# Earlier loads of C, a longer run of condition matmuls ahead of a stack, and other PSUM banks at the group boundary of a scan layer

## The chip, the core and the metric

The kernel runs on one core of a Trainium2 chip. The metric is the time of one execution in microseconds of the device. Five engines work side by side and wait for each other through semaphores: TensorE (PE, with its weight loads as PEld), VectorE (DVE), ScalarE (ACT), GpSimd (POOL) and SyncE (SP), which issues most of the DMAs.

## The reference, cut to what matters

The input x has 32 batches of 64 steps and 1024 channels. The layer is

```
c   = x @ W + lora(x)                     # "cond", gathered adapters, 1024 x 1024
dt, B, C = projections of c               # dt of 1024 channels, B and C of 16 states
h_t = exp(dt*A) * h_(t-1) + dt*B*c        # 16 states of each channel, 64 steps
y   = sum over states(h_t * C_t) + D*c
x1  = x + y
out = x1 + gated low-rank delta of (x1 @ W2 + bias + lora)
```

The part that the change touches is the scan `h` and the product `h * C`.

## The kernel before

The 32 batches are cut into 8 **groups** (G0 to G7) of 4 batches, that is 256 tokens. A group has 8 channel blocks `j` of 128 channels, and a block has 4 **units** `un`, each 8 states by 128 tokens. A place in the order is written (j, un), and a group has 32 of them, 256 in all. At each unit

- PE makes `dBx` (function `b_times_dtx`, four matmuls of `Bd` with `stacked`) in one of two PSUM buffers; it waits until the scan two units back is done;
- DVE scans it into `h` (L1011); it waits for `dBx`, for the decays `dA` (ACT, L612), and, `h` having two slots, for the product of two units back;
- POOL multiplies `h` by `Cb`, which is C spread over all partitions, into `hC` (L578);
- PE sums `hC` of three units back over the states (`sum_states`, L1214, eight transposing matmuls into bank `yp[j % 2]`, called "Y").

All the rest is cut into **jobs** that a table gives to a unit: `JOBS` for G1 to G5, `FIRST` for G0, `SIXTH` (jobs of at most the next group) for G6 and `FINAL` for G7. A job has a PSUM bank: "A" and "B" are `jb[0]` and `jb[1]`, "Y" is the `yp` of the block. PE does the jobs of a unit in the order of the list, after `b_times_dtx` and `sum_states` of that unit. It waits before the first matmul of a job until the bank's last tenant has been read. ACT does its part of a `stack`, `dtz` or `cond` one unit later (`LATE_ON_ACT`), DVE its part of a `dtz` one unit later (`LATE_ON_DVE`), its part of a `stack` or `xr` at the same unit, after the scan.

The jobs at the boundary:

- `cond` i of a later group, by chunks of k: three matmuls of 256 columns for each of 8 chunks, then one with the adapter (and, for i = 0, it needs `low`, which comes out of `xr`). Blocks 2m and 2m+1 share bank A.
- `dtz` i: two matmuls, then a softplus (ACT L593, L595, L597) and a max-add on DVE (L813) give the **step size** `dt` of two blocks.
- `xr`: 16 matmuls, then DVE L914 makes `low`.
- `stack` i: two transposes of `dtx` (made by POOL, L558, after the `hC` of the unit in the table `DTX`: `dtx` 8 at (6,3), 9 at (7,0), 2 at (0,0)). ACT copies them (L637), DVE subtracts (L906), SP writes them out (`put_dtx`, L421, 256 KB), waits for the landing, and at the next unit reads them back as `stacked` (`stack_dtx`, L428, three loads of 128 KB). `stack` 8 and 9 are blocks 0 and 1 of the next group.
- `b_diagonals` (DVE L829) makes `Bd` of the next group, at (6,3), (7,1), (7,3) and (0,1).

C of the next group is written to DRAM by SP at (6,2) (`put_c`, four DMAs, L406) and read back, spread over the partitions, by `spread_c` (L416): one load of 512 KB for each `un`. `Cb` has four slots, one for each `un`, so the load of slot un waits for the last `hC` of the group before that reads it, at (7, un). The loads of un 0, 1 and 2 are issued at (7,1), (7,2) and (7,3), that of un 3 at (0,1) of the next group. POOL waits for each of them at the first four units of a group. SP does everything in one order, so a wait in it holds what stands behind.

Of the kernel before, what the change touches and what calls it, by code (L numbers as in the profile page):

```python
# [4 lines left out]
P = 128  # L5
# [16 lines left out]
ROWS = 3 * Q  # L22
NDA, NH, NHC, NDT = 2, 2, 4, 4
PARTS = ((0, 0), (0, 1), (1, 0))
# [9 lines left out]
def job(name, i, bank, ks=None, ahead=None):  # L34
# [34 lines left out]
    (6, 3): [],  # L69
    (7, 0): [job("xr", 0, "Y", (0, 4)), job("xr", 0, "Y", (4, 8)), job("stack", 8, "B")],  # L70
    (7, 1): [job("cond", 0, "A", (0, 4), 2), job("dtz", 5, "Y")],
    (7, 2): [job("cond", 0, "A", (4, 8), 2), job("stack", 9, "B")],
    (7, 3): [job("cond", 1, "A", (0, 1), 2)],
}
# [29 lines left out]
    (6, 3): [],  # L104
    (7, 0): [job("xr", 0, "Y", (0, 4)), job("xr", 0, "Y", (4, 8)), job("stack", 8, "B")],
    (7, 1): [job("cond", 0, "A", (0, 4), 2), job("dtz", 5, "Y")],
    (7, 2): [job("cond", 0, "A", (4, 8), 2), job("stack", 9, "B")],
    (7, 3): [job("cond", 1, "A", (0, 1), 2)],
}
# [13 lines left out]
LORA_A, LORA2, LORA_B, LORA2_B = range(4)  # L123
ADAPTERS = {(1, 2): LORA2_B, (3, 0): 0, (4, 0): 1, (5, 2): 2}
DIAGONALS = {(0, 1): 3, (6, 3): 0, (7, 1): 1, (7, 3): 2}


def layer_kernel(nc, x, ids1, ids2, W, loraA, loraB, A_log, Dw, xproj_w, dtproj_w, dtproj_b,
# [6 lines left out]
    with ctx:  # L135
# [40 lines left out]
        Bd = sb("Bd", [P, NQ, R, Q], fr)  # L176
        Cb = sb("Cb", [P, UNITS, UNIT])
        x1 = sb("x1", [P, 2, TT, D])
# [27 lines left out]
        def xT_of(part, i):  # L206
# [4 lines left out]
               x1T[:, 4:8, :].rearrange("p k t -> p (k t)"), x1[:, 0, 0, :], x1[:, 0, 1, :], hC[:, 1, :], hC[:, 2, :], hC[:, 3, :]]  # L211
        Wraw = [Cb[:, :, :].rearrange("p u c -> p (u c)").rearrange("p (k o) -> p k o", k=K // 2),
                dA[:, :, :].rearrange("p h c -> p (h c)").rearrange("p (k o) -> p k o", k=K // 2)]
# [119 lines left out]

        def times_C(un):
            return (hC[:, un % NHC, :].rearrange("p (n b t) -> p b n t", n=HS, b=2),
                    h[:, un % NH, :].rearrange("p (b n t) -> p b n t", n=HS, b=2),
                    Cb[:, un, :].rearrange("p (b n t) -> p b n t", n=HS, b=2))

# [25 lines left out]
        def _(sp_e):  # L364
# [46 lines left out]
            def spread_c(G, un):  # L411
                if un == 0:
                    wait(sp_e, cscr_out, 64 * G + 64)
                wait(sp_e, hC_made, UNITS * K * G - UNITS + un + 1)
                src = c_scratch[G]
                sp_e.dma_start(Cb[:, un, :], src[un:un + 1, :].to_broadcast([P, UNIT])).then_inc(C_in[un], 16)  # L416

# [57 lines left out]
            def body(G, par):  # L475
                last = G == GROUPS - 1
                first = G == 0
                two_more = G + 2 < GROUPS
                for j in range(K):
                    t = K * G + j  # L480
                    for un in range(UNITS):
                        if un == 0:
                            load_xres(G, j, t)
                        if (j, un) == (0, 1) and not first:
                            spread_c(G, UNITS - 1)
                        which = ADAPTERS.get((j, un))
                        if which == LORA2_B:
                            load_lora2_b(G)
                        elif which == LORA2:
                            load_lora2(G)  # L490
                        elif which == LORA_A and two_more:
                            load_lora_a(G + 2)
                        elif which == LORA_B and two_more:
                            load_lora_b(G + 2)
                        for name, i, g, gpar, psum in ended_before(G, par, j, un):
                            if name == "stack":
                                stack_dtx(g, i)
                        for name, i, g, gpar, psum in ended_at(G, par, j, un):
                            if name == "stack":
                                put_dtx(g, i)  # L500
                        for name, i, g, gpar, psum in ended_at(G, par, j, un):
                            if name == "Bst":
                                put_c(g)
                            if name == "out":
                                store(g, i)
                        if j == K - 1 and un >= 1 and not last:

                            spread_c(G + 1, un - 1)

# [11 lines left out]
        def _(pool):  # L521
# [44 lines left out]
            def body(G, par):  # L566
                first, final = (G == g for g in (0, GROUPS - 1))
                for j in range(K):
                    for un in range(UNITS):
# [7 lines left out]
                        ns = slice(0, HS // 2 if s + 1 == UNITS * K * GROUPS else HS)  # L577
                        pool.tensor_tensor(*(x[:, :, ns, :] for x in times_C(un)), ALU.mult).then_inc(hC_made, 1)  # L578
                        if (j, un) in DTX and not (final and DTX[j, un] >= K):
# [229 lines left out]
        def _(dve):  # L809
# [218 lines left out]
            dve.wait_ge(C_in[UNITS - 1], 16 * GROUPS)  # L1028
            dve.tensor_tensor(*(x[:, :, HS // 2:, :] for x in times_C(UNITS - 1)), ALU.mult).then_inc(last_half, 1)
            add_residual(G, G % 2, K - 1, K * GROUPS - 1)  # L1030
# [312 lines left out]
```

## Time and profile before

| | us |
|---|---|
| median of 3 runs | 911.11 |
| lowest and highest | 909.5 and 913.29 |
| the profiled execution, its own time | 908.23 |
| its span, first to last instruction | 906.0 |
| busy: PE, DVE | 806.1 (89%), 764.7 (84%) |
| busy: POOL, ACT | 688.2 (76%), 643.4 (71%) |

The profile is of one execution, which was 2.9 us shorter than the median. 2.2 us of its time lie outside of the span. TensorE's granted clock was 0.968 of 2.4 GHz on the mean. The loop over the groups runs from 69.3 us to 885 us. A group takes 102.7 to 105.9 us from its first scan to that of the next one, G6 101.1.

### The profile page before, as it was taken

To read this page: it belongs to the slowest core of one execution; us is meant where nothing else is said; L and a number is where in the kernel's file an instruction comes from. 1 tells how busy PE (TensorE), PEld (TensorE's weight loads), DVE (VectorE), ACT (ScalarE), POOL (GpSimd) and SP (SyncE) were. 2 spreads that over 40 slices of the span, in tenths; PEclk is the share of its full clock that TensorE was granted. 3 is DMA by queue.
4 is the path that set the end of the run, shared out by engine and by line. 5 is a ranking of instruction groups with operands and counts; after the bars stand their busy time and mean duration, and the time that the engine had idled before them with its cause. 6 is when DMAs were issued, how large, how long until landed. Compare 5 with 4: busy or idle time off the path is not lost.

```text
span 906.0 us, 18640 instructions
## 1 busy us (share of the span) xinstructions
PE 806.1 (89%) x6416; PEld 770.7 (85%) x6416; DVE 764.7 (84%) x688; ACT 643.4 (71%) x1489; POOL 688.2 (76%) x349
## 2 busy tenths in 40 slices
PE   5988999899988999799988999799998999578784
PEld 4988998889978998799988998799987899567772
DVE  3447789888997899898998899988998799999993
ACT  4656678677775877777786886778776786779750
POOL 2016788788787888888878887788878898799891
PEclk9997999999998999999999999999999999899998
DMA  9988777366656557475675757375664754253221
GB/s 251 388 329 268 233 238 211 135 218 184 211 160 226 190 170 238 122 273 149 206 214 178 247 158 247 121 251 167 213 192 148 221 172 141 70 163 101 88 64 47
DMA packets 103113, 172.24 MB, mean 190 GB/s; under 512 B 21865, under 2 KB 71657, under 8 KB 94830
## 3 DMA queue, kind: packets, MB, share of 16 engines
q1 hardware_dynamic: 85614, 94.12, 34.1%
q10 hardware_dynamic: 17408, 76.95, 24.7%
q8 instruction: 53, 0.87, 0.4%
q14 instruction: 38, 0.31, 0.1%
HBM read 137.33 MB, written 33.69 MB: 189 GB/s over the span
## 4 chain that ended last, share of the span: by engine, by line
PE 52%; POOL 12%; DVE 11%; issue 10%; ACT 9%; DMA 5%; SPq 0%; POOLq 0%; ACTq 0%; DVEq 0%
PE jb L1047 24%; PE yp L1214 13%; POOL hC L578 10%; PE dBx L1047 7%; DVE h L1011 6%; ACT dA L612 4%; PE jb L1051 3%; PE yp L1047 3%; DMA Cb<-c_scratch 2%; POOL dtx L558 2%; DMA dtx_scratch<-HL 1%; DVE Bd L829 1%; DMA x<-in_x 1%; PE yp L1051 1%; PE yp L1219 1%
## 5 line engine op out<-in xcount | busy, mean ns | idle before, releaser
L578 POOL TENSOR_TENSOR hC<-h,Cb 128x1024 f32<-128x1024 f32 (+1 forms) x256 | 632.5, 2475 | 145.0 <-DVE h L1011 130.6
L1011 DVE TENSOR_TENSOR_SCAN h<-dA,dBx 128x1024 f32<-128x1024 f32 x256 | 583.4, 2281 | 62.1 <-PE dBx L1047 50.3
L612 ACT ACTIVATE dA<-dt,negA 128x252 f32<-128x252 f32 x1024 | 430.3, 494 | 75.5 <-DVE h L1011 65.2
L1214 PE MATMUL yp<-ident,hC 128*128 128x128 f32 x2048 | 274.7, 278 | 16.7 <-DVE HL L906 8.0
L1214 PEld LDWEIGHTS yp<-ident,hC 128*128 128x128 f32 x2048 | 236.7, 144 | 20.7 <-issue 11.4
L1047 PE MATMUL jb<-xT,Wst 128*128 128x256 f32 x1416 | 215.7, 296 | 0.0
L1047 PE MATMUL dBx<-Bd,stacked 96*128 96x256 f32 x1024 | 186.1, 304 | 12.8 <-DVE h L1011 6.2
L1047 PEld LDWEIGHTS jb<-xT,Wst 128*128 128x128 f32 x1416 | 186.2, 195 | 1.9
L1047 PEld LDWEIGHTS dBx<-Bd,stacked 96*128 96x128 f32 x1024 | 146.2, 195 | 18.8 <-issue 15.6
L558 POOL TENSOR_TENSOR dtx<-dt,u 128x256 f32<-128x256 f32 x64 | 54.2, 847 | 39.2 <-DVE dt L813 39.2
L647 ACT ACTIVATE u<-jb 128x512 f32<-128x512 f32 x31 | 18.6, 599 | 33.1 <-PE jb L1047 30.7
L829 DVE TENSOR_TENSOR Bd<-Bhl,diag 96x1024 fp32r<-96x1024 f32 x32 | 38.6, 1208 | 0.1
L1047 PE MATMUL jb<-low,GB 128*128 128x256 f32 x128 | 38.2, 379 | 0.0
L910 DVE TENSOR_TENSOR xT<-jb,xT 128x512 fp32r<-128x512 f32 x26 | 17.8, 684 | 21.3 <-ACT xT L641 21.1
L1219 PE MATMUL yp<-ident,Du 128*128 128x128 f32 x128 | 35.7, 279 | 0.0
L639 ACT ACTIVATE x1T<-jb 128x512 f32<-128x512 f32 x32 | 19.1, 596 | 22.4 <-PE jb L1051 21.7
L1047 PE MATMUL jb<-G,x1T 128*128 128x132 f32 x256 | 33.7, 279 | 1.0 <-ACT x1T L639 0.7
L641 ACT ACTIVATE xT<-jb 128x512 fp32r<-128x512 f32 x26 | 15.5, 596 | 26.8 <-PE jb L1051 26.2
L1051 PE MATMUL jb<-ident,dtx 128*128 128x128 f32 x48 | 9.7, 284 | 26.0 <-POOL dtx L558 26.0
L1047 PEld LDWEIGHTS jb<-G,x1T 128*128 128x128 f32 x256 | 30.8, 190 | 1.8 <-ACT x1T L639 0.9
L603 ACT ACTIVATE Du<-u,Dsb 128x256 f32<-128x256 f32 x64 | 31.6, 496 | 0.0
L1047 PE MATMUL jb<-u,xprojT 128*128 128x256 f32 x128 | 30.5, 381 | 0.7 <-ACT u L647 0.7
(173 smaller groups left out, 735.3 us busy)
## 6 DMA issues: line engine op xcount, KB each, us to landing
Wst<-W_scratch ACTq DMA_DIRECT2D x54, 1024.0 KB, 5.9
stacked<-dtx_scratch SPq DMA_DIRECT2D x192, 128.0 KB, 2.6
dtx_scratch<-HL SPq DMA_DIRECT2D x64, 256.0 KB, 3.1
Cb<-c_scratch SPq DMA_DIRECT2D x32, 512.0 KB, 5.7
xres<-in_x SPq DMA_DIRECT2D x64, 128.0 KB, 4.3
out<-obuf SPq DMA_DIRECT2D x32, 256.0 KB, 3.9
xin<-in_x ACTq DMA_DIRECT2D x26, 256.0 KB, 5.2
GB<-in_L_cond_lora_B SPq DMA_DIRECT2D x64, 64.0 KB, 5.6
```

Source lines behind the costliest of these rows:

```text
L558: pool.tensor_tensor(dtx[:, i % 2, :], dt[:, i % NDT, :], u[:, i % K, :], ALU.mult).then_inc(dtx_made, 1)
L578: pool.tensor_tensor(*(x[:, :, ns, :] for x in times_C(un)), ALU.mult).then_inc(hC_made, 1)
L603: act.activation(Du[:, i % 4, :], u[:, i % K, :], ACT.Copy, scale=Dsb[:, i % K:i % K + 1]).then_inc(Du_made, 1)
L612: act.activation(dA[:, half % NDA, :].rearrange("p (b n t) -> p b n t", b=GB_, n=HS)[:, :, n, 1:STEPS], dt[:, j % NDT, :].rearrange("p (b ...
L639: act.activation(x1T[:, 2 * i:2 * i + 2, :].rearrange("p k t -> p (k t)"), psum[:, :], ACT.Copy).then_inc(taken[name], 1)
L647: act.activation(u[:, i - 1:i + 1, :].rearrange("p k t -> p (k t)"), psum[:, :], ACT.Copy).then_inc(taken[name], 1)
L829: dve.tensor_tensor(Bd[0:ROWS, NQ // 2 * p:NQ // 2 * (p + 1), HS * half:HS * (half + 1), :], Bhl[0:ROWS, NQ // 2 * p:NQ // 2 * (p + 1), HS ...
L1011: dve.tensor_tensor_scan(h[:, un % NH, :], dA[:, half % NDA, UNIT * p:UNIT * (p + 1)], dBx[un % 2][:, :], 0.0, ALU.mult, ALU.add).then_inc ...
L1047: return pe.matmul(o, lhsT, rhs, start=start, stop=stop, **kw)
L1051: return pe.matmul(o, in_, ident[first:first + n, first:first + n], is_transpose=True, start=True, stop=True)
L1214: last = pe.matmul(y, hC[:, un % NHC, P * n:P * (n + 1)], ident[:, :], is_transpose=True, start=un == 0 and n == 0, stop=False, skip_group ...
L1219: last = pe.matmul(y, Du[:, j % 4, P * p:P * (p + 1)], ident[:, :], is_transpose=True, start=False, stop=True, skip_group_check=True)
```

## The change

`Cb` gets seven slots, used in a ring: unit un of group G has slot (4G + un) mod 7. The loads of the next group are issued at (6,3) (un 0 and 1), (7,0) (un 2) and (7,1) (un 3), each after the other SP work of its unit. The wait of a load is that of the slot's reader in the ring: for un 0 to 2 a product of a whole group ago, for un 3 the product at (7,0). The load at (0,1) is gone. At (7,0) the two halves of `xr` go to bank B instead of Y, then come five chunks of `cond` 0, which used to stand at (7,1), and then `stack` 8, now in bank Y instead of B. `dtz` 5 at (7,1) goes to bank B instead of Y, with one chunk of `cond` 0 behind it (before it were four); (7,2) has two chunks instead of four; `stack` 9 moves from (7,2) to (7,3), behind the one chunk of `cond` 1, in bank B as before. G6 has neither `xr` nor the chunks, but does have `stack` 8 in Y, `dtz` 5 in B and `stack` 9 at (7,3). A scratch area that the build reserves for DMA is halved, which makes room for the slots.

```diff
-NDA, NH, NHC, NDT = 2, 2, 4, 4
+NDA, NH, NHC, NDT, NCB = 2, 2, 4, 4, 7
...
# in JOBS and in FIRST alike
-    (7, 0): [job("xr", 0, "Y", (0, 4)), job("xr", 0, "Y", (4, 8)), job("stack", 8, "B")],
-    (7, 1): [job("cond", 0, "A", (0, 4), 2), job("dtz", 5, "Y")],
-    (7, 2): [job("cond", 0, "A", (4, 8), 2), job("stack", 9, "B")],
-    (7, 3): [job("cond", 1, "A", (0, 1), 2)],
+    (7, 0): [job("xr", 0, "B", (0, 4)), job("xr", 0, "B", (4, 8)), job("cond", 0, "A", (0, 5), 2), job("stack", 8, "Y")],
+    (7, 1): [job("dtz", 5, "B"), job("cond", 0, "A", (5, 6), 2)],
+    (7, 2): [job("cond", 0, "A", (6, 8), 2)],
+    (7, 3): [job("cond", 1, "A", (0, 1), 2), job("stack", 9, "B")],
...
+SPREAD = {(6, 3): (0, 1), (7, 0): (2,), (7, 1): (3,)}
...
-        Cb = sb("Cb", [P, UNITS, UNIT])
+        Cb = sb("Cb", [P, NCB, UNIT])
...
+        def C_slot(G, un):
+            return (UNITS * G + un) % NCB
...
-                wait(sp_e, hC_made, UNITS * K * G - UNITS + un + 1)
+                s = UNITS * G + un - NCB
+                if s >= 0:
+                    sp_e.wait_ge(hC_made, UNITS * K * (s // UNITS + 1) - UNITS + s % UNITS + 1)
                 src = c_scratch[G]
-                sp_e.dma_start(Cb[:, un, :], src[un:un + 1, :].to_broadcast([P, UNIT])).then_inc(C_in[un], 16)
+                sp_e.dma_start(Cb[:, C_slot(G, un), :], src[un:un + 1, :].to_broadcast([P, UNIT])).then_inc(C_in[un], 16)
...
-                        if (j, un) == (0, 1) and not first:
-                            spread_c(G, UNITS - 1)
...
-                        if j == K - 1 and un >= 1 and not last:
-
-                            spread_c(G + 1, un - 1)
+                        for ahead in SPREAD.get((j, un), ()) if not last else ():
+                            spread_c(G + 1, ahead)
...
-    nc = _bacc.Bacc("TRN2", target_bir_lowering=False, num_devices=1, dynamic_dma_scratch_size=1024)
+    nc = _bacc.Bacc("TRN2", target_bir_lowering=False, num_devices=1, dynamic_dma_scratch_size=512)
```

## Rows read from the trace of the kernel before

**Rows 1.** Waits of all engines: who waited for whom, us in total, times, longest
```profile
PE jb L1051 <- POOL dtx L558: 26.0, 7, 6.8
...
POOL hC L578 <- DMA Cb<-c_scratch: 4.8, 3, 2.9
```

**Rows 2.** Timeline of PE, boundary of G3 and G4: start, us, what
```profile
472.86 2.15 PE L1047 MATMUL yp<-xT,GAs 128*128 128x256 f32 x16
477.97 0.41 PE L1051 MATMUL jb<-ident,dtx 128*128 128x128 f32 x2 [2.96 <-POOL dtx L558]
...
480.25 2.60 PE L1047 MATMUL jb<-xT,Wst 128*128 128x256 f32 x12
...
488.17 0.64 PE L1047 MATMUL dBx<-Bd,stacked 96*128 96x256 f32 x4
...
489.44 2.03 PE L1047 MATMUL jb<-xT,Wst 128*128 128x256 f32 x15
...
497.87 0.41 PE L1051 MATMUL yp<-ident,dtx 128*128 128x128 f32 x2 [1.48 <-POOL dtx L558]
```

**Rows 3.** A stretch: us, busy of PE, PEld, DVE, ACT, POOL, then PEclk, DMA share
```profile
478.00:484.00 6.00, 6.00 (x39) 6.00 (x40) 4.18 (x5) 3.20 (x8) 5.34 (x3) 0.72 0.33 107
```

**Rows 4.** Timeline of DVE there; L1011 are the scans, from (7,1) to (0,0)
```profile
474.86 0.68 DVE L813 SCALAR_TENSOR_TENSOR dt<-jb,dt 128x512 f32<-128x512 f32 x1
...
479.18 2.28 DVE L1011 TENSOR_TENSOR_SCAN h<-dA,dBx 128x1024 f32<-128x1024 f32 x1
...
483.60 2.29 DVE L1011 TENSOR_TENSOR_SCAN h<-dA,dBx 128x1024 f32<-128x1024 f32 x1 [1.03 <-PE dBx L1047]
...
487.30 0.42 DVE L906 TENSOR_TENSOR HL<-jb,HL 128x256 fp32r<-128x256 f32 x1 [0.82 <-ACT HL L637]
487.64 0.41 DVE L819 TENSOR_TENSOR x<-yp,xres 128x256 f32<-128x256 f32 x1
487.97 2.28 DVE L1011 TENSOR_TENSOR_SCAN h<-dA,dBx 128x1024 f32<-128x1024 f32 x1
...
491.28 2.27 DVE L1011 TENSOR_TENSOR_SCAN h<-dA,dBx 128x1024 f32<-128x1024 f32 x1
```

**Rows 5.** Timeline of DVE, boundary of G6 and G7: the scans (7,1) and (0,0)
```profile
787.88 2.29 DVE L1011 TENSOR_TENSOR_SCAN h<-dA,dBx 128x1024 f32<-128x1024 f32 x1
...
797.95 2.27 DVE L1011 TENSOR_TENSOR_SCAN h<-dA,dBx 128x1024 f32<-128x1024 f32 x1
```

**Rows 6.** Landing of three loads of stacked, issued at 481.5; then at 274.8
```profile
DMA to landing us min/median/max: 2.4/2.9/3.9
...
DMA to landing us min/median/max: 2.4/2.6/5.3
```

**Rows 7.** Timeline of SP's queue, boundary of G3 and G4
```profile
479.35 0.34 SPq L421 DMA_DIRECT2D dtx_scratch<-HL  x1
481.53 1.26 SPq L428 DMA_DIRECT2D stacked<-dtx_scratch  x3
```

**Rows 8.** Stretches (0,0) to (3,0) of G2, G3, G1, G6; one in G7
```profile
282.63:321.61 38.98, 38.98 (x322) 38.34 (x321) 31.06 (x21) 25.80 (x61) 30.68 (x17) 0.93 0.62 208
388.54:424.32 35.78, 34.27 (x301) 33.42 (x300) 30.95 (x22) 27.80 (x65) 32.47 (x17) 1.00 0.65 218
178.00:214.44 36.44, 34.62 (x301) 33.46 (x300) 30.88 (x22) 27.94 (x65) 32.42 (x17) 1.00 0.66 210
696.81:733.42 36.61, 34.74 (x301) 33.48 (x300) 30.87 (x22) 27.97 (x65) 32.45 (x17) 1.00 0.69 218
806.60:810.00 3.40, 3.40 (x19) 3.40 (x18) 2.33 (x2) 2.17 (x5) 3.13 (x4) 0.50 0.31 109
```

**Rows 9.** Timeline of PE: dBx at (0,0) of G2; stack 2 in G7
```profile
281.40 1.20 PE L1047 MATMUL dBx<-Bd,stacked 96*128 96x256 f32 x4 [3.53 <-DVE Bd L829]
...
804.53 0.41 PE L1051 MATMUL yp<-ident,dtx 128*128 128x128 f32 x2 [2.46 <-POOL dtx L558]
```

**Rows 10.** The page, DMA issues: count, KB each, us to landing
```profile
Cb<-c_scratch SPq DMA_DIRECT2D x32, 512.0 KB, 5.7
```

## What the change does to the time: the prediction

> **What bounds the kernel now.** I read the page first, then the waits of all engines, then the timeline of PE, DVE and SP around one boundary, then stretches of equal content. The page has PE at 89% and no engine idle for long, so it names no single bound; the waits do better. The largest one of PE in the loop is that for `dtx` from POOL in front of a `stack` in a `jb` bank: 26.0 us in 7 times, that is one wait at each of the seven boundaries, the largest (6.8) in G6 where PE has least to do [rows 1]. The timeline of PE at the boundary of G3 and G4, which stands for those of G0 to G5, shows it: `xr` ends at 475.0, and PE does nothing until `stack` 8 at 477.97 [rows 2]. After that idle stretch the granted clock is at its lower level, 1.2 GHz, for some 3.4 us: the stretch 478 to 484 has a mean of 0.72, where 1.2 GHz all through would be 0.50, and 12 `cond` matmuls take 2.60 us there, while 15 of the same take 2.03 at 2.4 GHz [rows 2, 3]. So PE loses about 3.0 us of idle time and about 1.5 us to the clock at each boundary, 4.5 in all.
>
> What PE loses isn't yet what the kernel loses. The other clock to read is the chain of scans on DVE [rows 4]. From the scan at (7,1), 479.18, to the one at (0,0), 491.28, are 12.10 us. The scan at (7,2) stood 1.03 us waiting for `dBx` from PE, which was busy with the four slow chunks of `cond` 0, and L906 stood 0.82 us waiting for ACT, which had waited for PE. In G6, whose (7,1) and (7,2) have no chunks, but `dtz` 5, both stacks and the same DVE work, the same stretch takes 10.07 us, 787.88 to 797.95 [rows 5]. That is a chain of DVE alone, and it is the floor for what the change can reach.
>
> **The change part by part.**
>
> *Five chunks ahead of `stack` 8.* Fifteen matmuls, 2.03 us [rows 2], go into the 2.96 us in which PE waits. They need bank A, whose tenant `dtz` 4 is read by L813 from 474.86 to 475.54 [rows 4], so PE starts them at about 475.6 and ends at 477.6, before `dtx` is there (477.9). `stack` 8 is not later; the margin is 0.3 us, and below it each 0.1 us costs 0.1 us. What stays idle is 0.6 and 0.3 us, in two pieces, and no low clock should follow. Bank Y for `stack` 8 has been free since the residual of block 5, a unit before; `xr` in B finds it free.
>
> *Fewer chunks behind.* (7,1) has 3 `cond` matmuls instead of 12, (7,2) 6 instead of 12. PE's `dBx` for (7,2) then comes at about 481, and DVE goes by its own work: scan and diagonals 3.31 us (as 487.97 to 491.28), so (7,2) at 482.5 instead of 483.6. Then scan, L813 and L819: about 2.2 + 0.65 + 0.4 = 3.25, so (7,3) at 485.75 instead of 487.97. Then scan, diagonals and now L906, 3.31 + 0.35, so (0,0) at 489.4 instead of 491.28 [rows 4]. Gain: 1.9 us, where the row of G6 gives 2.03 [rows 5]. Bounds: 2.0 above; below, 1.0, if only the wait for `dBx` goes and L906 meets a late ACT at its new place.
>
> *`stack` 9 a unit later.* Its bank B waits for L813 of `dtz` 5, which ends at about 485.5, and PE may stand some 0.8 us there. It is needed at (1,0), four units on. The put follows at about 490 and the loads at about 492.5, with no C load beside them; 2.4 to 5.3 us to land [rows 6] leaves room before 501. Cost nothing. In G6 the move puts 0.35 us of L906 from (7,2) to (7,3), and I count +0.3 for it.
>
> *Does the gain last?* Behind (0,0), PE must reach `stack` 2 when `dtx` 2 is there, and `dtx` 2 hangs on the scan at (0,0) through POOL. PE had 1.48 us of idle time there [rows 2]; from `dBx` of (0,0) at 488.17 it needed 8.2 us to be ready. With `dBx` at 486 to 487 it is ready at 494.2 to 495.2, and `dtx` 2 comes at 496.0. So PE doesn't bind before, and behind it everything is relative to `stack` 2. Six boundaries (G0 to G5) give 6 x 1.9 = 11.4 us; bounds 6 to 12.
>
> *C earlier.* SP's waits at (6,3) are for `put_c` to land, some 2.5 us at a time when its next urgent work (the put of `dtx` 8, 479.35) is 6 us off [rows 7]. The stalls for C that it removes: POOL's named waits are 4.8 us in 3 times [rows 1], but most of it is made up by slack. From (0,0) to (3,0), where the jobs are the same, G3 (0.3 us of such a wait) takes 35.78 us, G1 (2.7) takes 36.44, G6 (2.9) 36.61 [rows 8]. So 0.7 + 0.8 = 1.5 us come back, and nothing in G2 to G5. Bounds 0 and 4.8.
>
> *`stack` 8 behind a C load.* This is the cost to weigh. The third C load is now issued about 0.4 us behind the put of `dtx` 8 and ahead of the three loads of `stacked`. Those had landed 3.9 us after the third issue at most, 486.2, with PE asking at 488.17 [rows 2, 6, 7]. PE would now ask at 486.0 (the wait for L813 to 485.5, then the two transposes of `stack` 9), but by the slack just worked out it may be kept until about 488. I take the C load to cost them 1 us (its 512 KB against their 384), so they land at about 487, at no price. Bounds: nothing, and 2.4 us more than the 5.3 which the boundary of G1 and G2 shows.
>
> By the Trainium skill's "DMA: Bandwidth & Descriptors", section "Queues, rings and completion order", each DMA engine takes descriptors in ring order, so all of the C load stands in front of the `stacked` loads. The trace before has no such order at this place; the rule makes rival 3 likelier.
>
> *Sum.* 908.23 of the profiled execution - 11.4 - 1.5 + 0.3 = 895.6. The median of the runs is 2.9 us above that execution, so 898.5. I add 2 us for boundaries where a load comes late or the clock falls once: 900.5. A difference under 0.5% (4.6 us) can't be told from none here.
>
> **Rivals.**
>
> 1. *The gap moves to `stack` 2.* PE keeps 4.5 us and the chain only 1.9, so 2.6 more stand somewhere: partly before `stack` 9 and `dBx` of (0,0), partly before `stack` 2. An idle stretch of 1.5 us there left the clock up in G1 to G6, one of 2.46 us in G7 was followed by 3.4 us at 0.50 [rows 8, 9]. Behind `stack` 2 scans wait for PE, so a low stretch there costs about 1.5 us, and takes back most of the 1.9. At all six: 908.23 - 6 x 0.4 - 1.5 + 2.9 = 907 to 908, no difference. For it: the sizes; against it: the idle time is split.
> 2. *More than the sum.* At the boundary of G1 and G2 a load of `stacked` took 5.3 us. PE waited 3.53 us for it, and from (0,0) to (3,0) G2 took 38.98 against 35.78 us, at a mean clock of 0.93; ahead of (0,0) I estimate 1.6 of the 3.53 as lost too [rows 6, 8, 9]. If the new order avoids this, 4.8 more: about 894.
> 3. *Slower: `stacked` behind the C load.* It decides from a landing 1.8 us later than the 486.2 of before, that is 488. If the loads land at 490, PE stands 2 us past its slack and the clock falls behind that, as with the 3.53 us wait at 281.4 [rows 8, 9]: 2 + 1.6 against a gain of 1.9, +1.7 us at each of six, -1.5 for C: about 920. Against it: a whole load of C takes 5.7 us to land [rows 10], and would be down at 485.5.
> 4. *It does nothing.* Bank A free too late, so that the chunks push `stack` 8 by what they save later. It takes a start after 476.5; L813 is a fixed 0.7 us behind the diagonals, so I see no cause. About 909.
> 5. *All that PE loses comes back.* If DVE's chain didn't cap it, 4.5 us at each of six boundaries: 908.23 - 27 - 1.5 + 0.3 + 2.9 = 883. Against it: the 10.07 us of G6, where PE had nothing to do at all [rows 5].
>
> The Trainium skill speaks for rival 5 and prices it much the same ("TensorE: Matmul & The Clock Gate", section "HAM oscillation — how this bites in real kernels"): time at the lower clock costs half of itself, and the wait ahead of it comes on top. For the 3.4 us here that is an estimate of 1.7 by the page, beside the 1.5 by the rows.
>
> **How the numbers follow.** Forecast 900.5 with 0.58, its own range 895 to 905; rival 1, with a part of the boundaries, 0.17; rival 2, 0.1; rival 3, 0.08; rival 4, 0.05; rival 5, 0.02. Faster by over 0.5% is below 906.6: the forecast, rivals 2 and 5 and a part of rival 1, 0.74. Within: most of rival 1, rival 4: 0.17. Slower: rival 3 and a bit of the unknown, 0.09. The range 893 to 909 leaves out rivals 3 and 5 and the ends.
>
> **What would show it.** Right: in PE's timeline 15 matmuls between `xr` and `stack` 8, no low clock at 478 to 482; (7,1) to (0,0) about 10.2 us; no wait of POOL for C; a wait before `stack` 2 of 1 to 2 us at full clock. Wrong: a wait of `dBx` at (0,0) for `stacked`; a low clock behind `stack` 2; `stack` 8 later against the scan at (7,0) than 2.5 us.

## The result, and the profile after

| | before | after |
|---|---|---|
| median, us (20 runs each) | 912.57 | 920.39 |
| lowest and highest | 907.13 and 917.38 | 910.66 and 927.92 |
| ratio of after to before, 95% | | 1.0068 [1.0044, 1.0091] |

The change makes the kernel 0.7% slower. The forecast was 900.5 us, its range 893 to 909: the time lies outside of it, at rival 3's 920. The four longest runs of after, those above 924 us, are left out of the ratio; with them the medians are 7.8 us, 0.9%, apart. The profiled execution of after took 927.92 us, 7.5 above its median; what is read from it below was also seen at the boundaries of other kernels, the twelfth above all, whose profiled execution took 922.87.

The page of after, span and busy times:

```profile
span 925.7 us, 18639 instructions
...
PE 817.6 (88%) x6416; PEld 780.4 (84%) x6416; DVE 764.2 (83%) x688; ACT 641.0 (69%) x1489; POOL 688.4 (74%) x349
```

DVE and POOL do the same work in the same time. PE has 11.5 us more of it for the same 6416 matmuls, and its granted clock was 0.948 on the mean, where it was 0.968. The waits say what the clock follows (who waited for whom, us in total, times, longest):

```profile
DVE h L1014 <- PE dBx L1050: 76.5, 79, 4.1
...
PE dBx L1050 <- DMA stacked<-dtx_scratch: 30.9, 9, 5.9
...
PE yp L1054 <- POOL dtx L561: 8.9, 8, 5.2
```

The wait that was to go, PE's for `dtx` in front of `stack` 8, was 26.0 us before [rows 1]. `stack` 8 is in bank Y now, so it is in the last row: 7.4 of these 8.9 us, and 5.25 of them in G6. POOL's wait for `Cb` (4.8 us before) isn't in the list any more. In their place stand 30.9 us in which PE waits for `stacked` to land, and 24.0 of these are six waits of 2.96, 5.40, 4.37, 5.88, 2.92 and 2.50 us at (0,0) of G1 to G6. DVE's wait for `dBx` has grown with it, from 50.3 us in 68 times to 76.5.

The timeline of PE at the boundary of G3 and G4 (start, us, what, idle time before), the counterpart of [rows 2]:

```profile
480.96 2.05 PE L1050 MATMUL jb<-xT,Wst 128*128 128x256 f32 x15 [1.16 <-DVE dt L816]
483.40 0.41 PE L1054 MATMUL yp<-ident,dtx 128*128 128x128 f32 x2 [0.39 <-POOL dtx L561]
...
490.82 0.44 PE L1054 MATMUL jb<-ident,dtx 128*128 128x128 f32 x2 [0.66 <-DVE dt L816]
497.14 1.20 PE L1050 MATMUL dBx<-Bd,stacked 96*128 96x256 f32 x4 [5.88 <-DMA stacked<-dtx_scratch]
498.13 1.91 PE L1217 MATMUL yp<-ident,hC 128*128 128x128 f32 x8
499.69 2.65 PE L1050 MATMUL jb<-xT,Wst 128*128 128x256 f32 x15
```

The first three lines are what was forecast: 15 chunk matmuls in 2.05 us, then `stack` 8 with 0.39 us of idle time, then `stack` 9 with 0.66. The fourth isn't. PE stands 5.88 us for `stacked`, and behind that four `dBx` matmuls take 1.20 us, where they took 0.64 before. A stretch that begins 3 us before the end of the wait shows the clock (us, busy of PE, PEld, DVE, ACT, POOL, then PEclk):

```profile
494.20:501.00 6.80, 3.86 (x18) 3.89 (x19) 2.83 (x3) 2.46 (x7) 2.68 (x2) 0.51 0.63 179
```

0.51 of 2.4 GHz is the level of 1.2 GHz nearly all through: the clock had fallen while PE stood. On DVE, the scans from (7,0) to (0,1), to be put beside [rows 4]:

```profile
480.83 2.27 DVE L1014 TENSOR_TENSOR_SCAN h<-dA,dBx 128x1024 f32<-128x1024 f32 x1
...
484.60 2.28 DVE L1014 TENSOR_TENSOR_SCAN h<-dA,dBx 128x1024 f32<-128x1024 f32 x1
...
487.91 2.28 DVE L1014 TENSOR_TENSOR_SCAN h<-dA,dBx 128x1024 f32<-128x1024 f32 x1
...
491.02 2.27 DVE L1014 TENSOR_TENSOR_SCAN h<-dA,dBx 128x1024 f32<-128x1024 f32 x1
...
498.37 2.29 DVE L1014 TENSOR_TENSOR_SCAN h<-dA,dBx 128x1024 f32<-128x1024 f32 x1 [3.63 <-PE dBx L1050]
...
502.86 2.29 DVE L1014 TENSOR_TENSOR_SCAN h<-dA,dBx 128x1024 f32<-128x1024 f32 x1 [2.20 <-PE dBx L1050]
```

(7,2), at 487.91, is 7.08 us behind (7,0) (before 8.14, the 483.60 of [rows 4] less the scan at (7,0), 475.46). (0,0), at 498.37, is 17.54 us behind it (before 15.82), and (0,1) 4.49 further on (before 2.46). From here on every boundary is told in this way, in us behind its scan at (7,0), and "at G3" means the boundary at the end of G3.

Why does `stacked` land so late? The issues of SP there and, in a second fence, ScalarE's (the counterpart of [rows 7]):

```profile
484.77 0.32 SPq L427 DMA_DIRECT2D dtx_scratch<-HL  x1
485.14 1.97 SPq L422 DMA_DIRECT2D Cb<-c_scratch  x1
488.33 1.27 SPq L434 DMA_DIRECT2D stacked<-dtx_scratch  x3
489.65 0.44 SPq L422 DMA_DIRECT2D Cb<-c_scratch  x1
```

```profile
488.49 0.33 ACTq L353 DMA_DIRECT2D Wst<-W_scratch  x1
```

The `stacked` loads, by tile, from issue to landing:

```profile
DMA to landing us min/median/max: 5.6/6.1/7.5
```

They took 2.4, 2.9 and 3.9 us before [rows 6]. Two transfers are new around them. One is the C load ahead, which the prediction weighed. The other is the line of ScalarE: the weights of `cond` 2, 128 partitions, 1 MB, into the half of `Wst` that `cond` 0 has just used. The load waits for the end of `cond` 0, and by ending `cond` 0 earlier the change brings it forward. Before, it was issued here:

```profile
486.45 0.33 ACTq L349 DMA_DIRECT2D Wst<-W_scratch  x1
```

That is 11.0 us behind the scan at (7,0), when the `stacked` loads had landed. Now it is 7.7, at all six boundaries, and the `stacked` loads are issued at 6.1 to 8.3. The table has the numbers of the two profiled executions at the six boundaries, worked out from the timelines:

| us behind the scan at (7,0) | before | after |
|---|---|---|
| third load of `stacked`, from issue to landing | 2.5, 5.3, 2.9, 3.9, 2.6, 2.5 | 5.8, 7.8, 6.9, 7.5, 5.8, 5.5 |
| all of `stacked` landed | 9.5, 14.6, 10.1, 10.8, 9.5, 9.5 | 13.0, 15.4, 14.4, 15.9, 12.9, 12.5 |
| weights of `cond` 2 issued | 11.0, 9.4, then 11.0 | 7.7 at all |
| scan (0,0) | 15.9, 16.2, 15.8, 15.8, 15.8, 15.9 | 14.4, 17.1, 16.0, 17.5, 14.6, 14.1 |
| scan (0,1) | 18.3, 21.8, 18.3, 18.3, 18.3, 18.3 | 18.9, 22.1, 21.1, 22.0, 18.7, 19.6 |
| scan (3,0) | 52.3, 55.2, 51.6, 51.6, 51.6, 52.5 | 52.3, 55.5, 54.5, 55.4, 52.1, 54.2 |

The six differences of the last line add up to 9.2 us; the medians are 7.8 apart. The two profiled executions are 19.7 apart. Of the rest, 6.5 us lie inside group G4, from (3,0) to (7,0), where the change moves nothing (see the last section). At G6, where no weights are loaded, `stacked` lands at 11.9 in after (10.9 before); PE waits 1.56 us for it, but the scan at (0,0) is at 14.13 as before.

### The profile page after: what moved, and what is told of

Read it like the earlier page. It is cut to its first block, busy times and chain, and to the rows that moved or that the text cites. A ratio compares the mean times of both kernels' runs of the same rounds, so it can differ in the third digit from the quotient of the medians.

```text
span 925.7 us, 18639 instructions
## 1 busy us (share of the span) xinstructions
PE 817.6 (88%) x6416; PEld 780.4 (84%) x6416; DVE 764.2 (83%) x688; ACT 641.0 (69%) x1489; POOL 688.4 (74%) x349
## 4 chain that ended last, share of the span: by engine, by line
PE 52%; DVE 10%; POOL 10%; ACT 9%; issue 9%; DMA 9%; SPq 1%; ACTq 0%; POOLq 0%; DVEq 0%
PE jb L1050 23%; PE yp L1217 14%; POOL hC L581 8%; PE dBx L1050 7%; DVE h L1014 5%; DMA stacked<-dtx_scratch 5%; ACT dA L615 4%; PE jb L1054 3%; PE yp L1050 3%; DMA dtx_scratch<-HL 2%; POOL dtx L561 1%; PE yp L1054 1%; DMA x<-in_x 1%; DVE HL L909 1%; DVE Bd L832 1%
## 5 line engine op out<-in xcount | busy, mean ns | idle before, releaser
L1014 DVE TENSOR_TENSOR_SCAN h<-dA,dBx 128x1024 f32<-128x1024 f32 x256 | 583.2, 2280 | 80.3 <-PE dBx L1050 76.5
L1217 PE MATMUL yp<-ident,hC 128*128 128x128 f32 x2048 | 278.5, 281 | 14.6 <-DVE HL L909 7.6
L1217 PEld LDWEIGHTS yp<-ident,hC 128*128 128x128 f32 x2048 | 240.7, 145 | 18.1 <-issue 10.9
L1050 PE MATMUL dBx<-Bd,stacked 96*128 96x256 f32 x1024 | 190.3, 309 | 38.2 <-DMA stacked<-dtx_scratch 30.9
L1050 PE MATMUL jb<-xT,Wst 128*128 128x256 f32 x1416 | 218.4, 298 | 4.7 <-DVE dt L816 4.7
L1050 PEld LDWEIGHTS jb<-xT,Wst 128*128 128x128 f32 x1416 | 188.5, 197 | 7.5 <-DVE dt L816 5.5
L1050 PEld LDWEIGHTS dBx<-Bd,stacked 96*128 96x128 f32 x1024 | 149.4, 198 | 45.3 <-issue 41.9
L561 POOL TENSOR_TENSOR dtx<-dt,u 128x256 f32<-128x256 f32 x64 | 49.2, 770 | 38.2 <-DVE dt L816 38.2
L640 ACT ACTIVATE HL<-yp 128x256 fp32r<-128x256 f32 x47 | 17.7, 377 | 31.1 <-PE yp L1054 30.9
L913 DVE TENSOR_TENSOR xT<-jb,xT 128x512 fp32r<-128x512 f32 x26 | 17.8, 684 | 22.2 <-ACT xT L644 22.0
```

Of the source, the lines that this page charges most:

```text
L561: pool.tensor_tensor(dtx[:, i % 2, :], dt[:, i % NDT, :], u[:, i % K, :], ALU.mult).then_inc(dtx_made, 1)
L1014: dve.tensor_tensor_scan(h[:, un % NH, :], dA[:, half % NDA, UNIT * p:UNIT * (p + 1)], dBx[un % 2][:, :], 0.0, ALU.mult, ALU.add).then_inc ...
L1050: return pe.matmul(o, lhsT, rhs, start=start, stop=stop, **kw)
L1217: last = pe.matmul(y, hC[:, un % NHC, P * n:P * (n + 1)], ident[:, :], is_transpose=True, start=un == 0 and n == 0, stop=False, skip_group ...
```

## The experiments

The recorded expectations go by letters. Theory W says that the weights load, which comes 3.3 us earlier, is enough to make the `stacked` loads late. Theory C says that the C load ahead of them is enough. Theory D was written down after the first four kernels: a `stacked` load is safe if it is issued well before the weights load, the C load ahead pushes it past that moment, and the earlier weights load pulls the moment forward, so it takes both. Other meanings of a letter are said in the expectation itself.

**One half each.** The first kernel is after with the job tables of before, so it has only the C part. The second is before with the new job tables, so four slots and C loads at their old places.

```diff
# C part alone: in JOBS and FIRST
-    (7, 0): [job("xr", 0, "B", (0, 4)), job("xr", 0, "B", (4, 8)), job("cond", 0, "A", (0, 5), 2), job("stack", 8, "Y")],
+    (7, 0): [job("xr", 0, "Y", (0, 4)), job("xr", 0, "Y", (4, 8)), job("stack", 8, "B")],
...
# jobs alone: the change's tables put into the kernel before, nothing else
```

> The seven slots and the early loads of C alone, with the old job tables. Theory W (the loads of stacked come late because the load of the next weights, 1 MB on ScalarE's queue, is issued 3.3 us earlier, as cond 0 ends earlier): the weights are loaded when they were before, so stacked lands at most 1 us later than before, inside the slack of PE, and only the waits for C go: 909 to 912, ratio 0.997 to 1.001. Theory C (the third load of C stands ahead of the loads of stacked in SP's ring): the loads of stacked come 3 us or more later, PE waits at (0,0): 913 to 918.

> The new job tables and banks alone, C in four slots and loaded as before. Theory W: the weights still come 3.3 us earlier, so dBx at (0,0) still waits 2 us or more for stacked at most boundaries, 914 to 920. Theory C: nothing stands ahead of the loads of stacked, so the gain of 1.9 us at each boundary comes: 900 to 905.

C alone: median 910.47, ratio 0.9989 [0.9958, 1.0019]. Jobs alone: 910.79, ratio 0.999 [0.9958, 1.0022]. Neither is slower, neither is faster. Theory C had 913 to 918 for the first, theory W had 914 to 920 for the second: neither transfer is enough alone, and the new order of PE's jobs by itself doesn't lose the time either. The halved scratch area, which the first kernel has too, costs nothing that shows. With C alone the `stacked` loads landed at 10.4 to 12.4, which is 0.4 to 1.7 us later than at the same boundary of before (G1 aside, which was disturbed there); PE asks for them at 12.7 or later, and no wait came out of it. The jobs alone are the better lesson, since their six boundaries fell into two kinds. (The profiled execution of this kernel took 923.15 us, 12 above its median, so the number of boundaries of each kind needn't be the usual one.) Here are SP's issues and, behind them, ScalarE's and the landing, at the boundary of G3 and G4:

```profile
484.75 0.34 SPq L421 DMA_DIRECT2D dtx_scratch<-HL  x1
488.15 1.27 SPq L428 DMA_DIRECT2D stacked<-dtx_scratch  x3
```

```profile
488.47 0.37 ACTq L349 DMA_DIRECT2D Wst<-W_scratch  x1
```

```profile
DMA to landing us min/median/max: 2.4/5.9/6.0
```

And one boundary on, SP's issues and the landing:

```profile
596.40 1.26 SPq L428 DMA_DIRECT2D stacked<-dtx_scratch  x3
```

```profile
DMA to landing us min/median/max: 2.4/2.5/2.6
```

The weights load is issued at 7.7 in both. At G4 the three loads go out at 6.1 to 7.0, ahead of it, and take 2.4 to 2.6 us; (0,0) comes at 13.8, 2.0 earlier than before. At G3 they go out at 7.3, 7.7 and 8.2: the first takes 2.4 us, the two that are issued beside or behind the weights load 5.9 and 6.0. G1 is of the second kind (6.7 us for the third load), and the other three of the first. What goes with the kind is the put of `dtx` 8, whose landing SP waits for before it issues the loads: 2.0 us from issue to landing at four boundaries, 2.9 and 3.2 at these two. So the weights load is a door: a `stacked` load that is issued some tenths of a microsecond ahead of it is quick, one behind it takes 6 us. By the Trainium skill's "DMA: Bandwidth & Descriptors", section "Issuing engines are not separate DMA queues", DMAs issued by the ScalarE and SyncE sequencers run on the same 16 DMA engines and interleave. The loads here agree with it: a 1 MB load on another engine's queue slows them from 2.4 to 6.0 us.

**Undo one of the two transfers in after.** The third kernel issues the third C load at (6,3) with the other two, so nothing stands between put and `stacked`. The fourth leaves C as in after and issues the weights of `cond` 2 at (0,0) instead of (7,3).

```diff
# third kernel
-SPREAD = {(6, 3): (0, 1), (7, 0): (2,), (7, 1): (3,)}
+SPREAD = {(6, 3): (0, 1, 2), (7, 1): (3,)}
```

```diff
# fourth kernel, on ScalarE
-                            if name == "cond" and i + 2 < K:
+                            if name == "cond" and i == 0 and (j, un) == (7, 3):
+                                pass
+                            elif name == "cond" and i + 2 < K:
                                 load_W(act, g, i + 2)
...
+                        if (j, un) == (0, 0) and 0 < G < GROUPS - 1:
+                            load_W(act, G + 1, 2)
```

> The changed kernel with the third load of C issued with the first two at (6,3), so that none stands between the put of dtx 8 and the loads of stacked. Theory W: the third load of stacked still takes 5 us or more, of the 8 us by which the changed kernel is slower at most 3 come back: 915 to 919. Theory C: 900 to 905.

> The changed kernel with the load of the weights of cond 2 issued one unit later, at (0,0) instead of (7,3), on ScalarE's queue. Theory W: stacked lands at about 10.5 us behind the scan at (7,0) instead of 12.5 to 15.9, the wait of dBx goes and the gain comes: 900 to 905. Theory C: the third load of C is still ahead, at most 2 of 8 us come back: 917 to 920.

The third gave 908.73, ratio 0.9971 [0.9939, 1.0004]; the fourth 901.37, ratio 0.9874 [0.9837, 0.9912]. Both undo the loss, and the fourth turns it into nearly the gain that was forecast. For the third, theory W had 915 to 919 and theory C 900 to 905, and both missed it; for the fourth, theory W had 900 to 905 and theory C 917 to 920. In the third, five boundaries of the profiled execution (899.75 us, its fastest) have `stacked` down at 9.5 to 10.3 and (0,0) at 13.8 (one at 14.5); at G3 the put took 3.57 us, the loads came behind the weights load (4.8, 6.1, 6.6 us), and PE waited 5.17. In the fourth, the weights go out at 10.5, `stacked` lands at 10.2 to 11.1, and PE waits 0.2 to 1.1 us for it. (0,0) is at 13.8 or 13.9 at all six, but in the profiled execution, 8 us above the median, (1,0) comes at 28.7, 27.6 and 27.1 at G0 to G2 instead of 26.1; more on this below.

**Both, and the controls.** The fifth kernel joins the two edits. The sixth also issues the fourth C load at (7,3). The seventh is the kernel before with late weights, the eighth the jobs alone with late weights.

> The changed kernel with the third load of C at (6,3) and the weights of cond 2 a unit later. Theory D (a door: the loads of stacked are safe if they are all in SP's ring well before the weights are issued; the C load ahead pushes them past it, the earlier weights pull it closed): with both taken away no dBx at (0,0) waits over 0.5 us, 7 boundaries at 13.8 us from the scan (7,0) to (0,0): 896 to 901. Theory W alone: as e4, 901, within 2 us.

> As e5, and the fourth load of C at (7,3) instead of (7,1), so that none stands close behind the loads of stacked either. Theory D: those already land within the slack of DVE's chain, so nothing more comes: within 2 us of e5. Theory B (the C load behind the third load of stacked costs too): 1 to 3 us below e5.

> The kernel before with only the weights of cond 2 a unit later. Control: there the loads of stacked land before the weights are issued at six of seven boundaries, so all theories expect no gain; if the later weights are themselves late for cond 2, it is slower: 910 to 914.

> The new job tables and banks with the weights a unit later, C in four slots and as before. Theory D: the gain of 1.9 us at each of six boundaries comes, only the waits for C stay or grow, as the scans come 2 us earlier and the last load of C does not: 900 to 905. Theory C (the early C loads are what the gain needs): 908 to 912.

| | median, us | ratio to before, 95% |
|---|---|---|
| fifth: no C load ahead, weights late | 897.62 | 0.9857 [0.9826, 0.9888] |
| sixth: also the fourth C load later | 901.23 | 0.9893 [0.9862, 0.9923] |
| seventh: before, weights late | 913.85 | 1.0025 [0.9998, 1.0051] |
| eighth: jobs alone, weights late | 909.16 | 0.9982 [0.9954, 1.001] |

The fifth has the lowest median of this study, 1.4% below the kernel before, in the 896 to 901 of theory D. Its boundary of G3 and G4, the scans on DVE from (7,0) to (0,0), then SP's issues, then the one of ScalarE:

```profile
464.98 2.27 DVE L1018 TENSOR_TENSOR_SCAN h<-dA,dBx 128x1024 f32<-128x1024 f32 x1
468.75 2.28 DVE L1018 TENSOR_TENSOR_SCAN h<-dA,dBx 128x1024 f32<-128x1024 f32 x1
472.06 2.28 DVE L1018 TENSOR_TENSOR_SCAN h<-dA,dBx 128x1024 f32<-128x1024 f32 x1
475.17 2.27 DVE L1018 TENSOR_TENSOR_SCAN h<-dA,dBx 128x1024 f32<-128x1024 f32 x1
478.82 2.27 DVE L1018 TENSOR_TENSOR_SCAN h<-dA,dBx 128x1024 f32<-128x1024 f32 x1
```

```profile
462.73 1.29 SPq L422 DMA_DIRECT2D Cb<-c_scratch  x3
...
468.93 0.32 SPq L427 DMA_DIRECT2D dtx_scratch<-HL  x1
472.06 1.27 SPq L434 DMA_DIRECT2D stacked<-dtx_scratch  x3
473.38 0.44 SPq L422 DMA_DIRECT2D Cb<-c_scratch  x1
```

```profile
475.46 0.33 ACTq L353 DMA_DIRECT2D Wst<-W_scratch  x1
```

From (7,1) to (0,0) are 10.07 us, to the hundredth what G6 showed before [rows 5]. The stretches from (7,0) to (3,0) show the whole of it, first that of before, then of after, then of the fifth kernel:

```profile
475.46:527.06 51.60, 47.61 (x399) 46.69 (x400) 44.13 (x34) 36.85 (x86) 44.50 (x23) 0.97 0.60 199
```

```profile
480.80:536.25 55.45, 48.36 (x399) 47.09 (x400) 44.16 (x33) 36.39 (x86) 44.51 (x23) 0.94 0.54 172
```

```profile
464.98:514.57 49.59, 46.73 (x399) 45.25 (x400) 44.09 (x34) 36.57 (x86) 44.65 (x23) 1.00 0.62 203
```

The same work takes 51.60, 55.45 and 49.59 us, and the clock is 0.97, 0.94 and 1.00. In the seventh kernel late weights are worth nothing, but it is a weak control: `cond` 0 ends so late there that the edit moves the load only from 11.0 to 11.2 at most boundaries. The eighth contradicts theory D, which had 900 to 905 for it. Its boundaries do have (0,0) at 13.8 or 13.9, all six of them, but the time is given back at the next units: the waits list of that kernel has

```profile
POOL hC L578 <- DMA Cb<-c_scratch: 13.9, 6, 3.0
```

where before it was 4.8 us in 3 times [rows 1]. With the scans 2 us earlier and the C loads at their old places, C is late, and (3,0) comes at up to 53.5. C isn't the only thing that is late. At (1,0) the trace shows a second meeting of the same kind. At five boundaries the `stacked` loads of `stack` 9 are issued at 18.2 to 20.4, behind the next weights load (that of `cond` 3, at 17.2 to 17.8), and the last of them lands at 26.3 to 27.4. PE waits 1.0 to 2.1 us for it, and (1,0) comes at 27.4 to 28.5 instead of 26.1. These waits are the larger part of this row:

```profile
PE dBx L1051 <- DMA stacked<-dtx_scratch: 10.7, 8, 2.1
```

Four boundaries of the second kernel, those that were 2.0 us earlier at (0,0), lost it in the same way: (1,0) is at 27.8 to 28.5. So the early C loads are needed, though by themselves (first kernel) they gave nothing that can be told from noise; how much of that is C itself and how much its traffic beside `stack` 9's loads isn't separated. The sixth kernel is 3.6 us above the fifth by the medians, outside the 2 us that theory D allowed; the intervals of the two ratios overlap. At two of its boundaries (1,0) comes at 27.4 and 26.9 instead of 26.1. There the later C load is in flight from 14.4 to 19.1 and 19.5, the weights of `cond` 3 take 8 us instead of 5, and the last load of `stack` 9 lands at 26.4 and 25.9 where the fifth kernel has 24.1 and 24.6. The fourth kernel's late (1,0) is of the same kind, with landings at 26.1 to 27.6.

**Traffic or order?** Two kernels ask what it is in the weights load that costs: its bytes, or that ScalarE issues it ahead of its decays. The ninth loads, at the old place, 16 of its 128 partitions (128 KB), and leaves the rest of these weights out. The tenth keeps all of it, behind the four decays of (7,3).

```diff
# ninth
+                            if name == "cond" and i == 0 and (j, un) == (7, 3):
...
+                                act.dma_start(W_chunk(2)[0:16, :], W_scratch[2][0:16, :]).then_inc(W_in[0], 16)
```

```diff
# tenth: no weights load at the end of cond 0, but behind the decays
                             decays(G if nj < K else G + 1, nj % K, nhalf, un % 2)
+                        if (j, un) == (7, 3) and G < GROUPS - 2:
+                            load_W(act, G + 2, 2)
```

> The changed kernel with the weights of cond 2 issued at the old place, (7,3), but only 16 of the 128 partitions of them in six groups (128 KB instead of 1 MB; cond 2 then multiplies what else lay in the buffer, so the output of these groups is not the reference's). All else, the order of ScalarE's instructions too, is that of the changed kernel. If the traffic of the weights is what delays the loads of stacked: 898 to 904, as with the late weights. If what e4 mended was the order on ScalarE: 915 to 920, as the changed kernel.

> The changed kernel with the weights of cond 2 issued in the same unit (7,3), but behind the four decays instead of ahead of them, 1.7 us later (at 9.4 us from the scan at (7,0)). Theory D: the loads of stacked, issued from 6.1 to 7.5 us on and landing at 10.2 to 11.0 without the weights, are caught by them only where they are late themselves: between e4 and the changed kernel, and nearer to e4: 901 to 908. If any weights load ahead of dBx at (0,0) does the harm: 912 to 920.

The ninth gave 906.1, ratio 0.9939 [0.991, 0.9968], 2 us above what traffic alone was to give and 9 below what order was. The issue is at 7.7 as in after, and `stacked` landed at 10.4 to 13.2, at G3 with

```profile
DMA to landing us min/median/max: 3.9/4.3/5.0
```

where after has 5.6, 6.1 and 7.5. The bytes are most of it. The rest isn't separated: this kernel still has the C load ahead and 128 KB of weights, and PE's waits at (0,0) are 0.3 to 3.1 us at the six boundaries. The tenth gave 922.75, ratio 1.0082 [1.0046, 1.0119], far from the 901 to 908 of theory D, because its premise fell. The weights load wasn't later at all (ScalarE's timeline, G3 and G4):

```profile
487.29 0.89 ACT L615 ACTIVATE dA<-dt,negA 128x252 f32<-128x252 f32 x2
487.86 0.33 ACTq L353 DMA_DIRECT2D Wst<-W_scratch  x1
488.08 1.29 ACT L615 ACTIVATE dA<-dt,negA 128x252 f32<-128x252 f32 x3
```

487.86 is 7.7 us behind the scan at (7,0), as in after. In the program the load now stands behind all the decays of (7,3), and yet the trace has six of the eight decays around it start after its issue (the window above cuts off three). The last matmul of `cond` 0 ends on PE at 487.82 here, at 488.46 in after, and the issue comes 0.04 and 0.03 us later. What sets the issue is the end of `cond` 0 on PE, not ScalarE's place in the order by four decays. So this kernel is a second copy of after, and agrees with it.

**Two more on the place.** If the end of `cond` 0 sets the door, one moved chunk is enough to move it. The eleventh kernel has the C loads of the third and the last chunk of `cond` 0 at (7,3), with ScalarE untouched. The twelfth asks whether the fourth C load, issued right behind the `stacked` loads in after, has a part in the loss: it puts it at (7,3).

```diff
# eleventh, in JOBS and FIRST, besides the SPREAD of the third
-    (7, 2): [job("cond", 0, "A", (6, 8), 2)],
-    (7, 3): [job("cond", 1, "A", (0, 1), 2), job("stack", 9, "B")],
+    (7, 2): [job("cond", 0, "A", (6, 7), 2)],
+    (7, 3): [job("cond", 0, "A", (7, 8), 2), job("cond", 1, "A", (0, 1), 2), job("stack", 9, "B")],
```

```diff
# twelfth
-SPREAD = {(6, 3): (0, 1), (7, 0): (2,), (7, 1): (3,)}
+SPREAD = {(6, 3): (0, 1), (7, 0): (2,), (7, 3): (3,)}
```

> As e3 (third load of C at (6,3)), and the last chunk of cond 0, with which its weights are done, at (7,3) instead of (7,2); no edit on ScalarE. The next weights then follow from the job table at about 10.5 us from the scan at (7,0) instead of 7.7. Theory D: as e5, 896 to 901. If only the edit on ScalarE's order did it: as e3, 907 to 911.

> The changed kernel with the fourth load of C at (7,3) instead of (7,1), so that it isn't issued at the same moment as the weights, right behind the loads of stacked. If it is the weights and the C load ahead that do the harm: 915 to 921, at most 3 us better. If the fourth load has a share of a third or more: 905 to 914.

The eleventh gave 899.65, ratio 0.988 [0.9831, 0.993]. The weights go out at 9.0, `stacked` lands at 9.6 to 11.0, and (0,0) is at 13.8 or 13.9 everywhere. That is in theory D's 896 to 901, and as good as moving the load itself, within what can be told. The twelfth gave 921.0, ratio 1.0094 [1.0057, 1.013], with this in its waits:

```profile
PE dBx L1050 <- DMA stacked<-dtx_scratch: 18.7, 5, 6.3
```

The fourth C load has no share in the loss that shows: 921.0 against 920.39.

## Why the prediction was wrong, and where it was right

The step that failed is "`stack` 8 behind a C load", the term taken at 1 us and no price. It weighed only what SP issues ahead of the `stacked` loads. It didn't count what another queue issues behind them: the chunks that the change moves ahead end `cond` 0 earlier, and the 1 MB weights load of ScalarE hangs on that end. The C load by itself did about what was written, 0.4 to 1.7 us later at no price (first kernel). The weights load by itself was harmless at (0,0) of four boundaries of six (second kernel). Together they shut the door in front of the third `stacked` load at every boundary, even at the three where it was issued 0.5 to 0.7 us ahead of the weights. That load took 5.5 to 7.8 us and landed at 12.5 to 15.9, where the prediction had about 487 (11.5 in this count) and called 488 (12.5) the point from which it decides. PE waited 2.5 to 5.9 us, and a step at 1.2 GHz followed.

Point by point:

- *Five chunks ahead of `stack` 8: right.* 15 matmuls of 2.05 us in the idle time, `stack` 8 at 2.57 us behind the scan at (7,0), no low clock there.
- *Fewer chunks behind: right.* (7,1) to (7,2) takes 3.31 us and (7,2) to (7,3) 3.11, forecast 3.3 and 3.25. With nothing in the way of `stacked` the whole is 10.07 (fifth kernel), forecast 10.2, and (0,0) is 2.0 us earlier, forecast 1.9. Six times that are 12 us.
- *`stack` 9 a unit later: right.* PE stands 0.66 us for its bank, forecast 0.8. In G6 the forecast +0.3 didn't show, (0,0) is at 14.13 as before (14.14). Its loads land in time in after. But where (0,0) is early they meet the weights of `cond` 3 (eighth kernel), which the cost of nothing left out.
- *Does the gain last: right, where it arises.* In the fifth kernel the mean clock from (7,0) to (3,0) of G3 and G4 is 1.00, so no low stretch follows `stack` 2, and (3,0) is at 49.6 or 49.7 at five boundaries and at 50.2 at the sixth. Rival 1 falls.
- *C earlier: alone neither its sign nor its size can be told.* 1.5 us was forecast; the medians of the first kernel and of before are 1.6 apart, with an interval that holds zero. But the gain of the jobs doesn't last without it: the eighth kernel, which has all of the fifth but the C part, is 11.5 us above it. So the terms don't add, which the sum didn't say.
- *Rival 3: right in place and time, half right in mechanism.* It had 2 us of standing and 1.6 of clock against a gain of 1.9. Against the fifth kernel, after loses on the mean of six boundaries 1.8 us up to (0,0) and 2.6 more up to (0,1), 4.4 in all, or 26 for the six; the medians are 22.8 apart. A chance of 0.08 was too low since only one of the two transfers that bear on it had been looked for.
- *Rival 2: the disturbed boundary of G1 and G2 in before* shows the same picture. There the put took 4.36 us, the loads were issued at 8.4, the weights load at 9.4, and the third load took 5.3. In the fifth kernel this boundary is like the others: (3,0) is at 49.6 instead of 55.2. The row with the 5.3 us was in the prediction [rows 6]; the weights load beside it on ScalarE's queue wasn't looked at.

The sum of the prediction was 898.5 before 2 us were added for late loads. The fifth kernel, the change without its two collisions, has 897.62. The arithmetic of the moved work was right, and what was missing was one DMA. That the two times agree to a microsecond is partly luck: the sum takes 12.6 us off, and the fifth kernel is 14.6 below the 912.18 of before in its own batch (13.0 by the ratio), with its third C load at another place and a before that is 1 us above the 911.11 that the sum started from.

## What to carry to other kernels

When work is moved earlier, list every DMA that waits for the end of that work, on every engine's queue, and see what small load with a deadline it will now share the DMA engines with. Where a small load decides, nothing of size should be issued in the microseconds around it, ahead or behind: here the large one issued 2.8 us later brought back 19 us, and issued 1.3 or 2.8 us later with the small load's other neighbour moved too, 21 to 23. A later place has its own neighbours, though: look at the next small load, as the fourth and the eighth kernel show at (1,0). And a change whose two halves are each neutral isn't therefore neutral, nor is a kernel that came out slower a reason to drop it: one line of its profile named the wait, and two small moves turned +0.7% into -1.4%.

## What was not expected of the hardware

- A load of 128 KB that is issued about 0.3 us ahead of a 1 MB load of another queue takes 2.4 to 2.7 us; issued 0.05 us or more behind it, 5.9 to 6.7 us (second kernel, G1 and G3). With one 512 KB load in flight ahead as well, the third load is already slow when issued 0.5 to 0.7 us ahead of the 1 MB (5.8 and 5.5 us, after). Without the weights load near, but with the C load, it takes 2.6 to 4.1 us (fourth kernel).
- With a C load in flight the first two `stacked` loads of after take 3.0 to 3.2 us at three boundaries of six, instead of 2.3 to 2.6 mostly; in the first kernel they take 2.6 to 3.1 at five and 3.5 and 4.0 at G3.
- The put of `dtx` 8 takes 2.0 us at most boundaries, but at G3 and G4 it takes 2.9 to 3.6 in all eleven profiled kernels with the new tables, and 2.0 in the three with the old ones; at G1 and G2 it is 2.3 to 3.0 against 2.0, 2.0 and 4.4. The cause is open; it made the difference between a boundary that gained and one that lost in the second and third kernels.
- The same meeting occurs inside a group, where the change moves nothing. In group G4 of after, ahead of the scan at (5,0), a put of `dtx` took 3.6 us instead of 2.6, so that the third `stacked` load was issued behind a weights load that goes out 8.0 us after the scan at (4,0) in both. It took 6.6 us instead of 2.6, PE waited 3.62 us, and the group became 6.5 us longer. The seventh kernel, with the old tables, shows it at the same place (PE waits 3.2 us), the fourth too (4.0).
- The clock fell to 1.2 GHz with a wait of PE of 2.5 us as well as with one of 5.9, in the longer ones while PE still stood; the step from (0,0) to (0,1) takes 4.1 to 5.4 us in after instead of the 2.2 of the fifth kernel. In the fourth kernel it fell behind a wait of 1.02 us at G1, and that step took 3.0.
